# Attention values in batches of three steps, with six probability tiles and a lead of 38 maxima products

## What is computed

```python
xn  = layernorm(x)
qkv = xn @ w_attn + b_attn            # 16 heads of 32
q, k = rope(q), rope(k)
s   = where(causal, q @ k^T, -inf)
o   = (softmax(s) * 512 ** -0.5) @ v
out = x + (o @ w_proj + b_proj) + experts(xn)   # 8 experts, top 2
```

## Time and profile before

| | us |
|---|---|
| median of 3 runs (lowest, highest) | 962.93 (962.67, 965.32) |
| the profiled execution | 965.8 |
| its span | 964.0 |
| PE busy | 864.3 (90%) |
| DVE, ACT, POOL busy | 361.3, 290.1, 281.6 |
| values L1365, maxima L1322, scores L1345 on PE | 147.3, 141.1, 138.0 |
| first unit of the maxima, last values | about 204, 543 |

### The profile page before, as it was taken

The page is one execution under the profiler, slowest core; times in us unless marked ns, Lnnn a source line. Parts: engine busy times, 40 slices in busy tenths (PEclk is TensorE's granted clock), DMA queues, the critical chain, the costliest instruction groups (busy, mean ns, idle before and its releaser), DMA issues. The chain is left out here.

```text
span 964.0 us, 12502 instructions
## 1 busy us (share of the span) xinstructions
PE 864.3 (90%) x3533; PEld 520.5 (54%) x3534; DVE 361.3 (37%) x1086; ACT 290.1 (30%) x612; POOL 281.6 (29%) x360
## 2 busy tenths in 40 slices
PE   3989999659999999999999479999999999999990
PEld 2768787535555555555554234456666666666650
DVE  5862433385566666666563002111111111111110
ACT  3131121104555655556556300022222222222210
POOL 5733200034233242321222133213333333333230
PEclk9989999857999999999999879999999999999995
DMA  9396785895556676555520279963333333333326
GB/s 324 135 303 200 249 259 207 257 221 168 157 150 160 188 191 153 151 120 128 133 77 14 63 246 377 347 195 61 65 65 67 63 65 65 65 64 65 65 34 194
DMA packets 90774, 147.30 MB, mean 153 GB/s; under 512 B 29552, under 2 KB 38256, under 8 KB 90672
## 3 DMA queue, kind: packets, MB, share of 16 engines
q1 hardware_dynamic: 42624, 68.83, 22.7%
q10 hardware_dynamic: 38688, 59.33, 22.1%
q0 software_dynamic: 9424, 18.69, 11.2%
HBM read 81.21 MB, written 61.15 MB: 148 GB/s over the span
## 5 line engine op out<-in xcount | busy, mean ns | idle before, releaser
L1229 ACT ACTIVATE probs<-scores_t 128x512 f32<-128x512 f32 (+3 forms) x384 | 163.5, 492 | 146.7 <-PE scores_t L1345 133.7
L855 PE MATMUL gu<-w,rows_t 128*128 x624 | 197.6, 459 | 3.5 <-ACT rows_t L784 3.5
L855 PEld LDWEIGHTS gu<-w,rows_t 128*128 128x128 f32 x624 | 115.1, 190 | 72.4 <-issue 22.7
L1322 PE MATMUL maxima<-k_stack,q_stack 96*128 96x512 f32 (+3 forms) x384 | 141.1, 387 | 14.0 <-DMA q_stack<-qk_hi 9.3
L1365 PE MATMUL o_acc<-probs,v_ones 128*64 128x512 f32 (+3 forms) x768 | 147.3, 505 | 1.1 <-POOL probs L1179 1.1
L1345 PE MATMUL scores_t<-q_stack,k_stack 98*128 98x512 f32 (+3 forms) x384 | 138.0, 385 | 7.9 <-DMA q_stack<-row_lo 5.9
L1254 DVE CUSTOM_DVE_ANT_0 masked_scores<-maxima,mask_m 128x128 f32<-128x128 f32 (+3 forms) x256 | 121.4, 485 | 24.8 <-PE maxima L1322 21.9
L1258 DVE TENSOR_REDUCE mx<-maxima 128x1 f32<-128x512 f32 x128 | 88.2, 689 | 88.7 <-PE maxima L1322 88.6
L1345 PEld LDWEIGHTS scores_t<-q_stack,k_stack 98*128 98x128 f32 x384 | 72.9, 192 | 70.3 <-issue 43.5
L873 PE MATMUL down<-w,hidden_t 128*128 (+1 forms) x234 | 107.0, 592 | 0.8 <-DVE hidden_t L829 0.8
L1322 PEld LDWEIGHTS maxima<-k_stack,q_stack 96*128 96x128 f32 x384 | 76.7, 202 | 34.9 <-DVE mx L1258 10.1
(11 more groups left out here) (147 smaller groups left out, 882.5 us busy)
## 6 DMA issues: line engine op xcount, KB each, us to landing
w<-in_w_t ACTq DMA_DIRECT2D x8, 1408.0 KB, 7.4
routed<-blank_row ACTq DMA_DIRECT2D x20, 514.0 KB, 6.5
rows<-routed SPq DMA_DIRECT2D x39, 256.0 KB, 4.2
qk_hi<-st_hi SPq DMA_DIRECT2D x32, 256.0 KB, 4.2
qk_lo<-st_lo SPq DMA_DIRECT2D x32, 256.0 KB, 5.2
q_stack<-qk_hi ACTq DMA_DIRECT2D x32, 256.0 KB, 4.3
k_stack<-qk_hi ACTq DMA_DIRECT2D x26, 256.0 KB, 5.0
v_all<-o_t SPq DMA_DIRECT2D x16, 384.0 KB, 2.3
```

The costliest lines, as they stand in the source:

```text
L855: last = nc.tensor.matmul(gu[r][j][:, 0:I], rows_t[r][:, k * P:(k + 1) * P], w1[:, bass.ds(e, 1), k, j * I:(j + 1) * I].rearrange("p o n - ...
L1229: nc.scalar.activation(probs[:, k % PR, h, 0:w], scores_t[e % RING][:, 0:w], ACT.Exp).then_inc(exp_done, 1)
L1322: nc.tensor.matmul(mb[at % RING][:, 0:w], q_st[i][0:3 * HD, h, t * P:(t + 1) * P], k_st[i][0:3 * HD, h, c * CH:c * CH + w], start=True, st ...
```

## The change

Two constants of `attend` change. The number of probability tiles, the slots of a window, the steps after which ScalarE copies the banks, and the slot of the turn follow from them.

```diff
-    LEAD = 36
+    LEAD = 38
-    BATCH = 2
+    BATCH = 3
```

## The result

| us | before | after |
|---|---|---|
| median (lowest, highest), 4 runs each | 962.8 (961.73, 965.32) | 1011.9 (1011.19, 1013.65) |
| the profiled execution, its span | 965.8, 964.0 | 1013.65, 1012.0 |
| turn 1 | 237.00 | 238.37 |
| from turn 1 to turn 14, 13 rounds | 263.35 | 306.05 |

The changed kernel is slower by the factor 1.0511 (95% interval 1.0485 to 1.0536). The forecast was 994, with a range to 1009: the sign came as forecast, and so did the wait for a maxima bank and the late row; the size did not, +49 in place of +31.

What follows compares the result with a forecast made beforehand. The prediction took attention as bound by TensorE's own order, plus a sometimes late row of maxima. Ring 14, row 14 and smaller parts 1, 1.5 and 0.5 sum to +31 on the median 962.93: 994 us, range 974 to 1009.

Steps and rivals of the forecast that it cites:

- Removed: 0.39 us a batch: Values batches in attention: four a round in place of six save 0.78 us a round, about 11 us over 14 rounds.
- The bank ring: Three maxima banks: unit 4 waits for row_lo, other units for banks; net +1.0 us a round, +14 (0 to +20).
- The row: Maxima row into q_stack, issued by SP behind sort_out: 1.71 us later, TensorE waits, +14 (0 to +18, upper end +28).
- I take 1.4 of the 1.71: Row's landing: assumed to move by 1.4 us of the issue's 1.71 us slip, lateness 21 us, +14.
- The upper end that I drew from v_ones: v_ones loaded ahead of the row, no longer behind: if it slows the row by 0.8 us more, +28.
- The clock: TensorE's clock falling to 1.2 GHz after waits in the attention: no term in the 31 us, only a rival.
- rival D: TensorE's clock falls to 1.2 GHz after waits in half the rounds: 21 us more, 1015; chance 0.11.
- Small parts: GpSimd's scaling behind bank 1's later copy +1, round 15's unhidden row +1.5, two more prologue units +0.5.
- A: Both new waits, for maxima banks and for the row, stand: +20 to +43, 983 to 1006; chance 0.60.
- B: Row lands with the loads' backlog, as before; only ring and small parts cost, +17, 980; chance 0.20.
- C: Banks come free in time and row is not held, so fewer batches decide: -11, 952; chance 0.06.

Runs made afterwards that it cites:

- experiment 8: Kernel before, batches of two, with LEAD 40, row_high after step 7 and SP's row issued ahead of sort_out: 965.7 us, ratio 1.0024.
- 9: Changed kernel with SP's row ahead of sort_out, LEAD 40 and bank 1's copy back after step 3: 964.7 us, ratio 1.0013.
- Experiment 4: Kernel before with LEAD 38 in place of 36 alone, batches of two: 969.4 us, ratio 1.0046.
- Experiment 1: Changed kernel with SP issuing the next round's row ahead of sort_out: 984.8 us, ratio 1.0225 to the kernel before.
- experiment 3: Kernel before with ScalarE's copy of bank 0 after step 9 in place of step 7, nothing else: 1021.5 us, ratio 1.0581.
- Experiment 14: Kernel before with FIRST_LOAD 2 in place of 4 alone, loads of q, k and v two steps earlier: 957.95 us, ratio 0.9938.
- experiments 2: Changed kernel with LOW_LAG 0 in place of 1, VectorE doing row_lo right behind unit 2: 1018.7 us, ratio 1.0537.
- Experiment 6: Kernel before with bank 0's copy after step 9 and six extra 512-column products ahead of TensorE's wait for the row: 998.7 us, ratio 1.0342.
- experiment 13: Changed kernel with LOW_LAG 0 and six extra 512-column products ahead of the wait for the row: 1010.6 us, ratio 1.0478.
- experiment 11: Changed kernel with six extra 512-column products ahead of the wait for the row: 1014.8 us, ratio 1.0517.
- experiment 7: Changed kernel with SP's row ahead of sort_out and LEAD 40 in place of 38: 971.7 us, ratio 1.0084.

## Why the prediction was right or wrong

**Removed: 0.39 us a batch. Right as far as shown.** The batch of 1536 columns was to take 2.72 us from its start to the next product's, and takes 2.72 where the row is in time (turn 14). Experiments 8 and 9 show that fewer batches don't pay for the waits that come with them.

**The bank ring: right, a little small.** Unit 4 was to wait 1.1 us and waits 0.93, at turn + 1.91. The round grows by 1.2 us where 1.0 was forecast: +16.8 in place of +14. Experiment 4 isolates the wait of unit 4.

**The row: right in its mechanism; its size is the first failed step.** It was to go out at + 3.68 and + 4.24 and goes out at + 3.86 and + 4.49, the copy starting at + 1.49 and not + 1.3. The step that failed is "I take 1.4 of the 1.71", +14: I let the landing absorb part of the shift, where the same table gave up to +18 for the whole. None of the shift was absorbed in the sum: landings of 49.7 against 49.8 us. The table with the real shift of 1.96 and the use at + 6.23 gives +20, and the later issues in five rounds bring it to the +21.3 measured. Experiment 1 (row first, same loads, no wait) and experiment 3 (late copy alone, 21.3 us between turn and use) show it from both sides. The Trainium skill ("DMA: Bandwidth & Descriptors", Issuing engines are not separate DMA queues) says that DMAs issued from ScalarE and SyncE run on the same 16 DMA engines and interleave. Experiment 14 agrees: with the same issue time and fewer loads beside it the row is in time in 12 of 13 rounds. The upper end that I drew from v_ones, which is now loaded ahead of the row, did not come.

**The clock: left out of the sum, the second failed step.** It stands at nothing in the 31 us, and rival D had it at 0.11 and +21 on top; it is there, at +6.8 (1.3 ahead of the use, 5.5 behind it). My "no run here shows it yet in this stage" was a misreading, for the kernel before has it, behind the use in the round of turn 2, which has one wait of 1.08 us for VectorE and no late row:

```profile
269.00 0.50 PE L1322 MATMUL maxima<-k_stack,q_stack 96*128 96x512 f32 x1 [1.08 <-DVE mx L1254]
```

```profile
263.98:280.20 16.22, 15.14 (x71) 8.57 (x70) 10.19 (x33) 8.46 (x19) 6.67 (x10) 0.89 0.53 149
```

, with two waits and 1.00, were poor evidence against it: the longer waits of the changed kernel and of experiments 2 and 3 are followed by half-level stretches in some rounds and not in others. Experiment 6 shows that work in place of the wait brings most of it back, and experiment 13 the same for its clock; experiment 11 shows that it doesn't where the ring's wait stays. The ring's wait alone is not enough, for experiment 4 has it 14 times and keeps 1.00. The Trainium skill ("TensorE: Matmul & The Clock Gate", HAM oscillation) warns that waits between bursts of products throttle TensorE again, and experiment 3 bears it out: there the clock costs 35.6 us, more than the row. I had given it too small a chance.

**Small parts.** GpSimd, +1 forecast: 1.4 us of waits, in rounds whose row is late anyway, so about nothing, and 7.0 once that cover is gone (experiment 7). Round 15, +1.5: +1.9. The prologue, +0.5: +1.4. Behind the last values, 0: +0.9. Two slips of arithmetic changed nothing: 965.8 + 31 is 996.8, not 996.6, and the lateness at a full shift, set against + 6.1, is 25.6, not 25.1.

**Rivals.** A, the forecast, had both waits right and its range, to 1006, wrong: the forecast was 7 us short on the row, 7 on the clock and 3 on the ring. B, landing with the backlog, is wrong: it asked for under 8 us of row wait, there are 18.5. C fell with both of its conditions.

## What to carry to other kernels

A constant that sets a batch can place more than the batch: here it moved a copy by two steps, and the small DMA that TensorE waits for stood behind that copy in another engine's program. Before changing it, list for each latency-critical transfer what its queue issues ahead of it; here putting the row first was worth 27 us in the changed kernel, moving the loads out from beside it 6 in the kernel before, and the batch itself nothing. And when a transfer slips, move its landing by the whole slip unless a trace shows otherwise, and count the clock behind each new wait of TensorE among the costs.

## What the runs showed of the hardware

- The level of TensorE's clock behind waits varies from round to round of one execution with the same order of work: after waits for the row up to 3.8 us long it was 0.72 to 0.88 behind the use in ten of 13 rounds of experiment 3, while in the changed kernel nine of 13 rounds kept 1.00 there. Experiment 4, with waits of 11.8 us in 14 for row_lo and none for the row, kept 1.00 in all. The place of the half-level stretch moved with six added products (experiment 11). What decides between these rounds stays open.
- An 8 KB write of a row into q_stack, from the same queue, took 2.3 to 6.1 us to land beside loads of q, k and v, and 1.8 us with none beside it (turns 14 and 15), but once 3.2 there (experiment 3, turn 14).
- VectorE's stand of 1.8 us in three rounds of experiment 8, which ends 2.04 to 2.06 us after the start of GpSimd's fifth scatter each time, was not explained.
